# Loading and turning the recurrence's parameters between slots of the first FFN's second stage

## The chip, the cores and the metric

One core of one Trainium2 chip. The metric is the device time of one execution in microseconds. The kernel before took 712.2 us (median of three runs, 710.3 to 714.72).

## The reference

x is [2, 2048, 256] in float32, 4096 tokens. The block is x + 0.5 FFN(ln(x)), then x + recurrence(ln(x)), then x + 0.5 FFN(ln(x)) with the same FFN weights. ln has no gain.

```python
def ffn(x, Wr, br, ln_g, ln_b, W1, b1, W2, b2):      # E = 8 experts, F = 1024
    probs = softmax(x @ Wr + br); gate = max(probs); idx = argmax(probs)
    xn = layernorm(x) * ln_g + ln_b
    h = relu(xn @ W1[idx] + b1[idx])
    return (h @ W2[idx] + b2[idx]) * gate

def recurrence(h, down_w, up_w, layers):             # 3 layers of width 64
    x = h @ down_w.T
    for cw, cb, wr, br, wi, bi, log_a, ow, nw in layers:
        xc = cb + causal_conv4(x, cw)
        r, i = sigmoid(xc @ wr.T + br), sigmoid(xc @ wi.T + bi)
        a = exp(8 * r * log_sigmoid(log_a))
        hs = scan(h = a * h + sqrt(max(1 - a*a, 0)) * i * xc)
        x = rms_norm(hs @ ow.T, nw)
    return x @ up_w.T
```

## The kernel before, in words

The five engines run programs of their own that meet at semaphores. Tokens are routed by expert: for four chunks of 1024 tokens, VectorE takes moments, TensorE the router's logits, VectorE chooses the expert and a place (`choose`, `place`), and POOL scatters the rows with indirect DMAs to regions of DRAM, one per expert (`routed_rows`). A slot is 128 such rows of one expert. The first FFN has up to 40 slots (32 of them always), the second as many again. For each slot SP loads the rows (`slot_rows`, tile pay) and the first-product weights (`slot_weights`, tile w_0 to w_2), VectorE normalises (`norm`), TensorE turns the two halves (`turn_input`), ScalarE applies gain and shift while it keeps them (`affine`, mn_t), TensorE makes the first product in four quarters (`first_product`, 32 instructions), ScalarE and VectorE activate a half each (`activate`), TensorE makes the second product of the slot before (`second_product`), VectorE finishes that (`finish`), and POOL stores it by an indirect DMA. TensorE's order in a slot is: turn the next slot's input, first product, second product of the slot before. In it, a slot's first product must wait for the weights and the affine input, its second for both activations and for VectorE's read of the product before.

The first FFN runs in two stages: slots 0 to 8 need the first two chunks alone, slots 9 and later need all four. Ahead of slot 0 stands the front: loads of x, routing of two chunks, the tables of what each slot holds (`tables`, `order_of_use`), and the third chunk's transposes. The other work is put beside the slots by tables of numbers, `beside(at)`: number k is done in the step k // 24, of which VectorE, ScalarE and POOL have two a slot (before and after its activation) and TensorE eight (after each quarter of a product). The slots of the second stage stand one step of a slot later than their number, so steps 36 and 37 are slot 17's. The recurrence is put beside slots 19 and later of the first FFN and early slots of the second.

The recurrence needs its parameters turned. In the front, SP's `load_parameters` (L412) issues 24 small loads between the large ones, with one expert's second weights (1 MB, L409) after each sixth, all counted by one semaphore, s_par: biases, norm vectors and the slots' own b1, ln_g and ln_b into rows of tile rec that are turned to tile vec; conv_w to lay; six blocks of gate and output weights, down_w and up_w to rec. VectorE zeroes rec for it (L719), waits for all 24 and centres down_w (`centre_down`, L770). TensorE's `parameters` (L1499) waits for all 24, makes the router's product with up_w, and turns 83 rows of vectors, nine blocks of weights, down_w and up_w. ScalarE's `parameters` (L1294) keeps them in vec, rec_t, down_t, up_t and up_r. After it stand the third chunk's logits: `logits` on TensorE, `keep_logits` on ScalarE (tile lg_t, L1330), `turn_logits` on TensorE (L1561), then `in_motion(4)`, products that only keep TensorE busy (L1670), and slot 0.

## Time and profile before

| | us |
|---|---|
| runs, median (lowest to highest) | 712.2 (710.3 to 714.72) |
| profiled execution, first to last instruction | 711.9 |
| TensorE busy | 657.2 |
| VectorE busy | 410.6 |
| ScalarE busy | 272.6 |
| POOL busy | 171.9 |

The profiled execution's own 711.9 us is the span that all rows count from. PE is TensorE's products, PEld its weight loads, DVE is VectorE, ACT ScalarE, SP the queue that issues most DMAs. In a timeline a row is one instruction or several alike (xN): its start, its length, and in brackets the idle time of the engine ahead of it with what ended it. "issue" is idle time with no wait the profile shows, "remote" a wait whose releaser it doesn't know.

### The profile page before, as it was taken

The page shows a single profiled execution, that of the slowest core. Times are in us where ns is not written, and L with a number is a line of the kernel's source. Part 1 is how long each engine was busy: PE and PEld are TensorE (multiplying, and loading weights), DVE is VectorE, ACT ScalarE, POOL GpSimd, SP SyncE. Part 2 cuts the span into 40 slices and gives each one's busy share as a digit, 9 for nine tenths or more (in the row PEclk, how much of TensorE's full clock was granted, in tenths as well). Part 3 has the DMA queues.
Part 4 walks back from the last instruction along what each step waited for, and adds up shares of the span by engine and source line. Part 5 has one row for each costly group of instructions (what it writes and reads, how often), then busy time and mean ns, then how long its engine had stood idle before and what let it go on. Part 6 is the DMA issues. An engine that isn't in the chain of part 4 may idle for free.

```text
span 711.9 us, 15541 instructions
## 1 busy us (share of the span) xinstructions
PE 657.2 (92%) x4420; PEld 576.8 (81%) x4420; DVE 410.6 (58%) x1427; ACT 272.6 (38%) x642; POOL 171.9 (24%) x177
## 2 busy tenths in 40 slices
PE   7549999899999999999998998999899999999993
PEld 5339998899988878898777867889689989999992
DVE  7556772333346586777887767787667633333331
ACT  3124221222245557554562536644443223222220
POOL 4723443011121120123312240124202521111111
PEclk9659999999999999999999999999999999999997
DMA  8969683955564462436416337323373466453530
GB/s 288 307 202 391 242 273 93 322 189 192 180 208 142 149 208 82 150 129 203 148 54 223 123 127 259 135 89 120 127 260 118 166 231 215 150 197 102 175 127 14
DMA packets 59919, 126.51 MB, mean 178 GB/s; under 512 B 8105, under 2 KB 36660, under 8 KB 59700
## 3 DMA queue, kind: packets, MB, share of 16 engines
q1 hardware_dynamic: 53204, 108.50, 45.7%
q0 software_dynamic: 6624, 16.92, 6.5%
q8 instruction: 42, 0.69, 0.4%
q14 instruction: 49, 0.40, 0.2%
HBM read 106.36 MB, written 20.35 MB: 178 GB/s over the span
## 4 chain that ended last, share of the span: by engine, by line
PE 66%; DVE 8%; issue 8%; DMA 6%; DVEq 3%; POOL 3%; another core or an unknown queue 2%; SPq 1%; ACT 1%; POOLq 0%; ACTq 0%
PE bank L1691 30%; PE bank L1705 26%; DMA pay<-routed_rows 3%; POOL routed_rows L633 2%; PE bank L1678 2%; DMA x_middle<-res,pay 2%; PE bank L1595 1%; DMA routed_rows<-rows,dest 1%; DVE st L746 1%; PE bank L1628 1%; PE bank L1533 1%; PE bank L1602 1%; DVE rec L1082 1%; PE bank L1561 1%
## 5 line engine op out<-in xcount | busy, mean ns | idle before, releaser
L1691 PE MATMUL bank<-mn_t,w 128*128 128x128 f32 x2368 | 287.7, 278 | 1.3 <-DVE act_t L1172 1.3
L1691 PEld LDWEIGHTS bank<-mn_t,w 128*128 128x128 f32 x2368 | 277.7, 195 | 11.3 <-issue 8.5
L1705 PE MATMUL bank<-w,act_t 128*128 x1184 | 274.8, 381 | 5.5 <-DVE y_b L1181 5.1
L1705 PEld LDWEIGHTS bank<-w,act_t 128*128 128x128 f32 x1184 | 217.3, 190 | 42.2 <-issue 16.5
L1417 ACT ACTIVATE mn_t<-bank,vec 128x128 f32<-128x128 f32 x152 | 61.4, 454 | 222.3 <-PE bank L1678 198.4
L1172 DVE TENSOR_SCALAR act_t<-bank,vec 128x128 f32<-128x128 f32 x296 | 83.3, 344 | 104.6 <-PE bank L1691 90.4
L1427 ACT ACTIVATE act_t<-bank,vec 128x128 f32<-128x128 f32 x296 | 84.9, 369 | 78.0 <-PE bank L1691 77.9
L642 POOL DMA_INDIRECT x_middle<-res,pay x37 | 36.9, 998 | 220.4 <-DVE res L1188 173.2
L1181 DVE TENSOR_TENSOR y_b<-bank,b_all 128x256 f32<-128x256 f32 x74 | 31.4, 425 | 97.5 <-PE bank L1705 85.4
L642 POOL DMA_INDIRECT out_x<-res,pay x37 | 36.5, 985 | 203.3 <-DVE res L1188 173.3
L633 POOL DMA_INDIRECT routed_rows<-rows,dest x64 | 64.7, 1011 | 55.9 <-PE bank L1691 27.2
L1163 DVE TENSOR_SCALAR mn<-pay 128x256 f32<-128x256 f32 x78 | 32.2, 413 | 21.6 <-DMA pay<-routed_rows 20.9
L625 POOL TENSOR_TENSOR inv_std<-var_eps,minus_half 128x16 f32<-128x16 f32 (+1 forms) x12 | 31.0, 2583 | 50.7 <-DVE var_eps L756 35.5
L1188 DVE SCALAR_TENSOR_TENSOR res<-y_b,pay 128x256 f32<-128x256 f32 x74 | 35.9, 485 | 7.2
L1678 PE MATMUL bank<-ident,mn 128*128 128x128 f32 x152 | 30.5, 283 | 8.2 <-DVE mn L1163 5.9
L746 DVE BATCH_NORM_STATS2 st<-rows 128x6 f32<-128x256 f32 x96 | 33.7, 414 | 2.6 <-DMA rows<-in_L_attn_h 0.7
L1678 PEld LDWEIGHTS bank<-ident,mn 128*128 128x128 f32 x152 | 20.4, 145 | 18.1 <-DVE mn L1163 6.4
L1321 ACT ACTIVATE xn_t<-bank 128x512 f32<-128x512 f32 x32 | 17.9, 600 | 26.9 <-PE bank L1533 20.2
L1058 DVE SCALAR_TENSOR_TENSOR rec<-seq,lay,rec 128x512 f32<-128x512 f32 x36 | 27.0, 749 | 2.0 <-issue 0.2
L1533 PE MATMUL bank<-ident,rows 128*128 128x128 f32 x128 | 20.7, 317 | 0.1
L1561 PE MATMUL bank<-pick,lg_t 128*128 128x16 f32 x64 | 8.9, 271 | 12.4 <-ACT lg_t L1330 12.4
L1359 ACT ACTIVATE rec<-bank,lay 64x512 f32<-64x512 f32 x24 | 16.4, 684 | 9.0 <-PE bank L1595 8.8
(212 smaller groups left out, 465.1 us busy)
## 6 DMA issues: line engine op xcount, KB each, us to landing
w<-in_L_ffn_W SPq DMA_DIRECT2D x82, 1024.0 KB, 7.3
pay<-routed_rows SPq DMA_DIRECT2D x78, 130.0 KB, 2.1
rows<-in_L_attn_h SPq DMA_DIRECT2D x8, 512.0 KB, 6.6
rows<-x_middle SPq DMA_DIRECT2D x8, 512.0 KB, 4.2
routed_rows<-fill SPq DMA_DIRECT2D x2, 1040.0 KB
routed_rows<-rows,dest POOLq DMA_INDIRECT x64
b_all<-in_L_ffn_b SPq DMA_DIRECT2D x1, 1024.0 KB, 10.7
x_middle<-res,pay POOLq DMA_INDIRECT x37, 2.5
```

The source lines that it names most:

```text
L633: g.indirect_dma_start(out=routed[f], out_offset=bass.IndirectOffsetOnAxis(ap=dest[:, t:t + 1], axis=0), in_=rows[:, t * RW:(t + 1) * RW], ...
L642: g.indirect_dma_start(out=x_out if p else x_mid, out_offset=bass.IndirectOffsetOnAxis(ap=pay[p][i % RING][:, C_ID:C_ID + 1].bitcast(I32), ...
L746: v.bn_stats(st[:, jj * 6:jj * 6 + 6], tile_of(c, b, j, 0, D))
L1163: v.tensor_scalar(mn[p][i % 2][:, :], a[:, 0:D], a[:, C_MEAN:C_MEAN + 1], a[:, C_RS:C_RS + 1], ALU.subtract, ALU.mult).then_inc(m_xn[p], 1)
L1172: last = v.tensor_scalar(act_t[i % 2][:, c * P:(c + 1) * P], b_hid[1][:, c % 4 * P:(c % 4 + 1) * P], vec[:, ds(eb + c, 1)], 0.0, ALU.add, ...
L1181: v.tensor_tensor(y_b[i % 2][:, :], b_out[i % 2], b2_all[:, ds(eb * (D // FC), D)], ALU.add).then_inc(m_yk[p], 1)
L1188: v.scalar_tensor_tensor(out=res[p][i % 2][:, :], in0=y_b[i % 2][:, :], scalar=a[:, C_GATE:C_GATE + 1], in1=a[:, 0:D], op0=ALU.mult, op1=A ...
L1417: last = a.activation(mn_t[p][i % 2][:, k * P:(k + 1) * P], b_in[i % 2][:, k * P:(k + 1) * P], ACT.Identity, scale=vec[:, V_G + k:V_G + k ...
L1427: last = a.activation(act_t[i % 2][:, c * P:(c + 1) * P], b_hid[0][:, c * P:(c + 1) * P], ACT.Relu, bias=vec[:, ds(eb + c, 1)])
L1678: last = t.transpose(b_in[i % 2][:, k * P:(k + 1) * P], mn[p][i % 2][:, k * P:(k + 1) * P], ident[:, :])
L1691: last = t.matmul(b_hid[half][:, c % 4 * P:(c % 4 + 1) * P], w1[i % W1S][:, k * F + c * P:k * F + (c + 1) * P], mn_t[p][i % 2][:, k * P:(k ...
L1705: last = t.matmul(b_out[i % 2], act_t[i % 2][:, c * P:(c + 1) * P], w2[:, ds(eb * (WE // FC) + c * D, D)], start=c == 0, stop=c == FC - 1)
```

## The change

Of the 24 loads the front keeps three: b1, ln_g and ln_b, the slots' own. They are turned (68 rows) and kept alone, in columns 0 to 67 of vec. The four experts' second weights are issued behind them in a row. The other 21 loads are issued three at a time by SP behind its work for slots 9 to 15. VectorE zeroes rec behind slot 7's activation and centres down_w behind slot 16's. TensorE turns the parameters between the first and the second quarter of slot 17's first product, into banks 4 to 7, and waits there for all 24 loads. ScalarE keeps them behind slot 17's activation. `layer_columns`, `exp_log_a` and `log_sigmoid` move from slots 0 to 3 to slot 18. The recurrence's first transposes wait for what ScalarE kept.

```diff
@@ -67,3 +67,7 @@
-LAYER_COLUMNS = 2
-EXP_LOG_A = 25
-LOG_SIGMOID = 72
+CLEAR_PARAMETERS = 360
+CENTRE_DOWN = 840
+TURN_PARAMETERS = 3456
+KEEP_PARAMETERS = 888
+LAYER_COLUMNS = 912
+EXP_LOG_A = 936
+LOG_SIGMOID = 937
@@ -215,2 +219,3 @@
-        assert RAW_D + 2 * D + P <= 3 * HC * CH
-        vec_rows = rec[0:NV, 3 * HC * CH - P:3 * HC * CH]
+        assert RAW_D + 2 * D + 2 * P <= 3 * HC * CH and LARGE * 2 <= 3 * HC * CH - P
+        vec_rows = rec[0:E * FC + 2 * KD, 3 * HC * CH - P:3 * HC * CH]
+        layer_rows = rec[0:5 * NL, 3 * HC * CH - 2 * P:3 * HC * CH - P]
@@ -374 +379,3 @@
-        N_PAR = 24
+        N_PAR, PER_SLOT = 21, 3
+        N_SLOT_PAR = 3
+        V_LAYERS = E * FC + 2 * KD
@@ -412 +419,5 @@
-            def load_parameters():
+            def load_slot_parameters():
+                for dst, src in ((vec_rows[0:E * FC, :], b1_in.rearrange("e (c p) -> (e c) p", p=P)),
+                                 (vec_rows[V_G:V_G + KD, :], ln_g.rearrange("(k p) -> k p", p=P)),
+                                 (vec_rows[V_B:V_B + KD, :], ln_b.rearrange("(k p) -> k p", p=P))):
+                    sp.dma_start(dst, src).then_inc(s_par, 16)
@@ -414 +425 @@
-                n_par = [0]
+            def parameter_loads():
@@ -416,9 +426,0 @@
-                def load(dst, src):
-                    sp.dma_start(dst, src).then_inc(s_par, 16)
-                    n_par[0] += 1
-                    if n_par[0] % 6 == 0:
-                        second_weights(n_par[0] // 6 - 1)
-                load(vec_rows[0:E * FC, :], b1_in.rearrange("e (c p) -> (e c) p", p=P))
-                load(vec_rows[V_G:V_G + KD, :], ln_g.rearrange("(k p) -> k p", p=P))
-                load(vec_rows[V_B:V_B + KD, :], ln_b.rearrange("(k p) -> k p", p=P))
@@ -427 +429 @@
-                        load(vec_rows[pos:pos + NL, b * DO:(b + 1) * DO], src)
+                        yield layer_rows[pos - V_LAYERS:pos - V_LAYERS + NL, b * DO:(b + 1) * DO], src
@@ -429,3 +431 @@
-                    load(lay_l[b * DO:(b + 1) * DO, :, 0:4], conv_w.rearrange("l c k -> c l k"))
-                sp.wait_ge(s_zero, 1)
+                    yield lay_l[b * DO:(b + 1) * DO, :, 0:4], conv_w.rearrange("l c k -> c l k")
@@ -435,2 +435,2 @@
-                        load(nat[b * DO:(b + 1) * DO, m, :, b * DO:(b + 1) * DO], src.rearrange("l o i -> o l i"))
-                load(rec[0:DO, RAW_D:RAW_D + D], down_w)
+                        yield nat[b * DO:(b + 1) * DO, m, :, b * DO:(b + 1) * DO], src.rearrange("l o i -> o l i")
+                yield rec[0:DO, RAW_D:RAW_D + D], down_w
@@ -439,2 +439,9 @@
-                    load(upn[:, :, b, :], up_w.rearrange("(k p) i -> p k i", p=P))
-                assert n_par[0] == N_PAR, n_par[0]
+                    yield upn[:, :, b, :], up_w.rearrange("(k p) i -> p k i", p=P)
+            def load_parameters(n):
+                for k, (dst, src) in enumerate(parameter_loads()):
+                    if k == 0 and n == 0:
+                        sp.wait_ge(s_zero, 1)
+                    if n * PER_SLOT <= k < (n + 1) * PER_SLOT:
+                        sp.dma_start(dst, src).then_inc(s_par, 16)
@@ -511,0 +519,2 @@
+                    if FIRST[0][1] <= i < FIRST[0][1] + N_PAR // PER_SLOT:
+                        load_parameters(i - FIRST[0][1])
@@ -565,2 +574,2 @@
-            load_parameters()
-            for e in range(N_PAR // 6, EAGER):
+            load_slot_parameters()
+            for e in range(EAGER):
@@ -719 +727,0 @@
-            v.memset(rec[:, 0:RAW_D], 0.0).then_inc(s_zero, 1)
@@ -771 +779 @@
-                dve.wait_ge(s_par, 16 * N_PAR)
+                dve.wait_ge(s_par, 16 * (N_SLOT_PAR + N_PAR))
@@ -1012,0 +1021,4 @@
+            def clear_parameters():
+                dve.drain()
+                v.memset(rec[:, 0:RAW_D], 0.0).then_inc(s_zero, 1)
@@ -1014 +1026 @@
-                dve.wait_ge(s_tpe, 1)
+                dve.wait_ge(s_tpe, 2)
@@ -1118,0 +1131,4 @@
+                    if k == CLEAR_PARAMETERS:
+                        clear_parameters()
+                    if k == CENTRE_DOWN:
+                        centre_down()
@@ -1277,3 +1293 @@
-            tables(0, 0, 0)
-            centre_down()
-            for part in range(1, 5):
+            for part in range(5):
@@ -1294 +1308 @@
-            def parameters():
+            def slot_parameters():
@@ -1296 +1310,5 @@
-                a.activation(vec[:, :], bank[0][:, 0:NV], ACT.Copy).then_inc(s_tpe, 1)
+                a.activation(vec[:, 0:V_LAYERS], bank[0][:, 0:V_LAYERS], ACT.Copy).then_inc(s_tpe, 1)
+            def parameters():
+                act.wait_ge(s_tp, 2)
+                a.activation(vec[:, V_LAYERS:NV], bk[0][0][:, 0:NV - V_LAYERS], ACT.Copy).then_inc(s_tpe, 1)
@@ -1298,3 +1316,3 @@
-                    a.activation(rec_t[:, m * NL * P:(m + 1) * NL * P], bank[1 + m][:, 0:NL * P], ACT.Copy)
-                a.activation(down_t[:, :], bank[0][:, P:P + KD * DO], ACT.Copy)
-                a.activation(up_t[:, :], bank[0][:, 2 * P:2 * P + D], ACT.Copy)
+                    a.activation(rec_t[:, m * NL * P:(m + 1) * NL * P], bank[5 + m][:, 0:NL * P], ACT.Copy)
+                a.activation(down_t[:, :], bk[0][0][:, P:P + KD * DO], ACT.Copy)
+                a.activation(up_t[:, :], bk[0][0][:, 2 * P:2 * P + D], ACT.Copy)
@@ -1303 +1321 @@
-                                        bank[1][b * DO:(b + 1) * DO, NL * P:NL * P + E], ACT.Copy)
+                                        bk[0][1][b * DO:(b + 1) * DO, NL * P:NL * P + E], ACT.Copy)
@@ -1383,0 +1402,2 @@
+                    if k == KEEP_PARAMETERS:
+                        parameters()
@@ -1488 +1508 @@
-            parameters()
+            slot_parameters()
@@ -1498,0 +1519,4 @@
+            def slot_parameters():
+                pe.wait_ge(s_par, 16 * N_SLOT_PAR)
+                t.transpose(bank[0][:, 0:V_LAYERS], vec_rows, ident[0:V_LAYERS, 0:V_LAYERS]).then_inc(s_tp, 1)
@@ -1500 +1523,0 @@
-                pe.wait_ge(s_par, 16 * N_PAR)
@@ -1501,0 +1525,2 @@
+                pe.wait_ge(s_par, 16 * (N_SLOT_PAR + N_PAR))
+                pe.wait_ge(s_kept[R1], NC)
@@ -1503 +1528 @@
-                    t.matmul(bank[1][:, NL * P:NL * P + E], rec[:, RAW_D + D + k * P:RAW_D + D + (k + 1) * P],
+                    t.matmul(bk[0][1][:, NL * P:NL * P + E], rec[:, RAW_D + D + k * P:RAW_D + D + (k + 1) * P],
@@ -1505 +1530 @@
-                t.transpose(bank[0][:, 0:NV], vec_rows, ident[0:NV, 0:NV])
+                t.transpose(bk[0][0][:, 0:5 * NL], layer_rows, ident[0:5 * NL, 0:5 * NL])
@@ -1509 +1534 @@
-                        t.transpose(bank[1 + m][:, l * P:(l + 1) * P], rec[:, o:o + P], ident[:, :])
+                        t.transpose(bank[5 + m][:, l * P:(l + 1) * P], rec[:, o:o + P], ident[:, :])
@@ -1512 +1537 @@
-                    t.transpose(bank[0][:, P + k * DO:P + (k + 1) * DO], rec[0:DO, RAW_D + k * P:RAW_D + (k + 1) * P],
+                    t.transpose(bk[0][0][:, P + k * DO:P + (k + 1) * DO], rec[0:DO, RAW_D + k * P:RAW_D + (k + 1) * P],
@@ -1515 +1540 @@
-                    last = t.transpose(bank[0][:, 2 * P + k * P:2 * P + (k + 1) * P],
+                    last = t.transpose(bk[0][0][:, 2 * P + k * P:2 * P + (k + 1) * P],
@@ -1520,0 +1546,3 @@
+                if (m, c, part) == (LN, 0, 0):
+                    pe.wait_ge(s_tpe, 3)
@@ -1634,0 +1663,2 @@
+                    if k == TURN_PARAMETERS:
+                        parameters()
@@ -1822 +1852 @@
-            parameters()
+            slot_parameters()
@@ -1825 +1855 @@
-            pe.wait_ge(s_tpe, 2)
+            pe.wait_ge(s_tpe, 1)
```

ScalarE in the front, before, from the third chunk's xn_t to slot 0's mn_t:

```order
L1321 ACTIVATE xn_t<-bank 128x512 [waits transposed0] x3
L1296 ACTIVATE vec<-bank 128x83 [waits param_transposed]
L1298 ACTIVATE rec_t<-bank 128x384 x3
L1299 ACTIVATE down_t<-bank 128x128
L1300 ACTIVATE up_t<-bank 128x256
L1302 ACTIVATE up_r<-bank 64x8 x2
L1330 ACTIVATE lg_t<-bank 128x512 [waits logits0,logits_turned0]
L1417 ACTIVATE mn_t_0<-bank,vec 128x128 [waits slot_transposed0,tables_ready]
```

And now:

```order
L1339 ACTIVATE xn_t<-bank 128x512 [waits transposed0] x3
L1310 ACTIVATE vec<-bank 128x68 [waits param_transposed]
L1348 ACTIVATE lg_t<-bank 128x512 [waits logits0,logits_turned0]
L1437 ACTIVATE mn_t_0<-bank,vec 128x128 [waits slot_transposed0,tables_ready]
L1437 ACTIVATE mn_t_0<-bank,vec 128x128
```

Seven copies have gone from between vec and lg_t.

TensorE at slot 17, before (mn_t_1 and w_2 are its input and first-product weights):

```order
L1678 MATMUL bank<-ident,mn_0 128x128 [waits slot_affine0,slot_normalised0]
L1678 MATMUL bank<-ident,mn_0 128x128
L1691 MATMUL bank<-mn_t_1,w_2 128x128 [waits activated_by_scalar0,slot_weights0_2,slot_affine0]
L1691 MATMUL bank<-mn_t_1,w_2 128x128 x7
L1691 MATMUL bank<-mn_t_1,w_2 128x128 [waits activated_by_vector0]
L1691 MATMUL bank<-mn_t_1,w_2 128x128 x7
L400 TENSOR_LOAD tab_b
```

And now:

```order
L1708 MATMUL bank<-ident,mn_0 128x128 [waits slot_affine0,slot_normalised0]
L1708 MATMUL bank<-ident,mn_0 128x128
L1721 MATMUL bank<-mn_t_1,w_2 128x128 [waits activated_by_scalar0,slot_weights0_2,slot_affine0]
L1721 MATMUL bank<-mn_t_1,w_2 128x128 x3
L1528 MATMUL bank<-wr_c,rec 128x8 [waits counts_kept0,params_loaded]
L1528 MATMUL bank<-wr_c,rec 128x8
L1530 MATMUL bank<-ident,rec 128x15
L1534 MATMUL bank<-ident,rec 128x128 x9
L1537 MATMUL bank<-ident,rec 128x64 [waits down_centred]
L1537 MATMUL bank<-ident,rec 128x64
L1540 MATMUL bank<-ident,rec 128x128 x2
L1721 MATMUL bank<-mn_t_1,w_2 128x128 x4
```

The router's product and the turns stand between the first quarter's four products and the rest, and wait for the loads and for the centring. SP at the end of its work for slot 15 and the start of slot 16's, before (w_0 takes slot 18's weights, pay_4 slot 19's rows, result_stored0_4 counts slot 14's store among others):

```order
L472 ISA [waits first_product_half0]
L472 DMA w_0<-in_L_ffn_W 128x2x1024
L461 TENSOR_LOAD tab_row
L461 ISA x2
L465 ISA [waits result_stored0_4]
L465 DMA pay_4<-routed_rows 128x260
L400 TENSOR_LOAD tab_b
L400 ISA x2
L472 ISA [waits first_product_half0]
```

And now:

```order
L479 ISA [waits first_product_half0]
L479 DMA w_0<-in_L_ffn_W 128x2x1024
L468 TENSOR_LOAD tab_row
L468 ISA x2
L472 ISA [waits result_stored0_4]
L472 DMA pay_4<-routed_rows 128x260
L447 DMA rec<-in_L_attn_down_w 64x256
L447 DMA rec<-in_L_attn_up_w 128x2x64 x2
L407 TENSOR_LOAD tab_b
L407 ISA x2
L479 ISA [waits first_product_half0]
```

The last three of the parameters' loads stand behind the load of slot 19's rows and ahead of slot 19's weights.

## Rows read from the trace of the kernel before

**Rows 1.** The page's head and its busy times by engine

```profile
span 711.9 us, 15541 instructions
...
PE 657.2 (92%) x4420; PEld 576.8 (81%) x4420; DVE 410.6 (58%) x1427; ACT 272.6 (38%) x642; POOL 171.9 (24%) x177
```

**Rows 2.** Busy time by stretch: PE, PEld, DVE, ACT, POOL; clock, DMA share, GB/s

```profile
26.00:42.00 16.00, 4.87 (x26) 3.10 (x26) 5.13 (x25) 1.05 (x2) 10.64 (x11) 0.68 0.69 236
42.00:51.00 9.00, 4.95 (x21) 4.46 (x22) 7.13 (x37) 3.44 (x11) 0.00 (x0) 0.50 0.78 247
51.00:80.00 29.00, 29.00 (x208) 26.87 (x207) 20.82 (x101) 11.29 (x32) 12.83 (x9) 0.92 0.92 330
...
170.00:200.00 30.00, 30.00 (x211) 28.15 (x211) 10.46 (x35) 8.09 (x25) 3.89 (x4) 1.00 0.55 189
```

**Rows 3.** TensorE's timeline in the front: start, us, what, idle before and its releaser

```profile
27.70 0.61 PE L1503 MATMUL bank<-wr_c,rec 128*128 128x8 f32 x4 [2.66 <-DMA rec<-in_L_attn_up_w]
...
30.77 0.69 PE L1515 MATMUL bank<-ident,rec 128*128 128x128 f32 x2
...
45.00 1.89 PE L1561 MATMUL bank<-pick,lg_t 128*128 128x16 f32 x8 [12.39 <-ACT lg_t L1330]
46.72 2.06 PE L1670 MATMUL bank<-ident 128*128 128x128 f32 x8
48.61 0.69 PE L1678 MATMUL bank<-ident,mn 128*128 128x128 f32 x2
...
50.80 1.92 PE L1691 MATMUL bank<-mn_t,w 128*128 128x128 f32 x8
```

**Rows 4.** ScalarE's timeline in the front

```profile
30.84 0.60 ACT L1321 ACTIVATE xn_t<-bank 128x512 f32<-128x512 f32 x1 [4.39 <-remote]
42.28 0.24 ACT L1296 ACTIVATE vec<-bank 128x83 f32<-128x83 f32 x1 [10.84 <-remote]
42.42 1.25 ACT L1298 ACTIVATE rec_t<-bank 128x384 f32<-128x384 f32 x3
...
44.35 0.60 ACT L1330 ACTIVATE lg_t<-bank 128x512 f32<-128x512 f32 x1
```

**Rows 5.** VectorE's timeline in the front

```profile
27.69 0.41 DVE L773 TENSOR_REDUCE mean_d<-rec 64x1 f32<-64x256 f32 x1 [1.56 <-DMA rec<-in_L_attn_up_w]
...
42.13 0.20 DVE L984 TENSOR_TENSOR beyond<-slot_e,jump_v 128x36 f32<-128x36 f32 x1 [2.12 <-issue]
...
48.18 0.38 DVE L1163 TENSOR_SCALAR mn<-pay 128x256 f32<-128x256 f32 x1
```

**Rows 6.** Timelines of POOL and of SP's queue in the front

```profile
38.71 0.98 POOL L633 DMA_INDIRECT routed_rows<-rows,dest  x1 [0.30 <-issue]
...
21.19 0.61 SPq L417 DMA_DIRECT2D rec<-in_L_attn_down_w  x1
21.84 1.15 SPq L417 DMA_DIRECT2D rec<-in_L_attn_up_w  x2
...
42.83 3.65 SPq L465 DMA_DIRECT2D pay<-routed_rows  x4
```

**Rows 7.** Timelines in slots 16, 17 and 19 of the second stage

```profile
176.51 3.74 PE L1691 MATMUL bank<-mn_t,w 128*128 128x128 f32 x32
...
180.40 1.12 DVE L1172 TENSOR_SCALAR act_t<-bank,vec 128x128 f32<-128x128 f32 x4 [2.40 <-PE bank L1691]
180.95 0.35 SPq L465 DMA_DIRECT2D pay<-routed_rows  x1
...
183.76 3.74 PE L1691 MATMUL bank<-mn_t,w 128*128 128x128 f32 x32
183.85 0.42 DVE L1181 TENSOR_TENSOR y_b<-bank,b_all 128x256 f32<-128x256 f32 x1 [2.33 <-PE bank L1705]
...
204.42 1.04 PE L1533 MATMUL bank<-ident,rows 128*128 128x128 f32 x8
```

**Rows 8.** Loads of a slot's rows from 130 to 200 us, issue to landing

```profile
DMA to landing us min/median/max: 2.0/2.1/4.8
```

2 lines of the change are left out of this document (1 added, 1 removed).

## The prediction

> **What bounds the kernel now.** I read the page's totals first, then the busy time by stretch, then the timeline of each engine through the front, and last one slot of the first FFN's second stage. TensorE is busy 657.2 of 711.9 us [rows 1]. By stretch it is full from 51 us on: 29.00 of 29 between 51 and 80, and 30.00 of 30 between 170 and 200, where VectorE works 10.46 and ScalarE 8.09 of the 30 and the DMA engines are 0.55 busy. Between 26 and 42 it works 4.87 of 16 us and from 42 to 51 4.95 of 9 [rows 2]. So there are two prices. An instruction put on TensorE inside the second stage costs its whole length, one put there on VectorE or ScalarE costs nothing while they keep their slack. In the front, only what makes the first slot's work start sooner is worth anything.
>
> What holds that start? TensorE turns the parameters from 27.70 to 31.46, after a wait for the last of 24 small loads, then makes the third chunk's logits, and stands still until 45.00, waiting for ScalarE's lg_t. Then it turns the logits, runs its idle-filling products from 46.72, turns slot 0's input at 48.61 and begins the first product at 50.80 [rows 3]. ScalarE keeps its last xn_t at 30.84, idles 10.84 us for which the profile has no known releaser, copies vec at 42.28 and rec_t from 42.42, and reaches lg_t only at 44.35 [rows 4]. VectorE, beside it, waited 1.56 us for the parameters before centring down_w at 27.69, has gaps of its own (2.12 us before 42.13, by "issue"), and normalises slot 0 at 48.18 [rows 5]. The third string is the rows themselves: POOL issues its last scatter at 38.71, and SP the first loads of slot rows at 42.83 [rows 6].
>
> **The change part by part.**
>
> *Front, ScalarE.* Removed between vec and lg_t: seven copies, from 42.42 to 44.35, 1.93 us [rows 4]. If the 10.84 us stay as they are, lg_t starts at 42.42, 1.9 us sooner, and since turning the logits and the filler follow it with no gap, slot 0's input can be turned at 46.7 [rows 3]. That needs slot 0 normalised by then.
>
> *Front, VectorE.* It loses the 1.56 us wait and centring, two passes of some 0.41 us [rows 5], so 2.4 us; slot 0's norm comes at 45.8 even if every gap stays. Slot 0's rows, issued at 42.83 [rows 6], take 2.1 us in a quiet stretch [rows 8], 44.9. Both are ahead of 46.7. The memset ahead of VectorE's first load wait is gone too, and was hidden by that wait.
>
> *Front, TensorE.* The router product and thirteen turns leave a stretch in which it waits for ScalarE anyway: worth nothing. One transpose, now of 68 rows, stays.
>
> *Front, SP and DMA.* 21 issues leave the queue, the dearest being down_w (0.61) and up_w (1.15 for two) [rows 6]. The first four experts' second weights and the fourth chunk of x are issued back to back. With the small packets gone from among them, these large loads are through a little sooner. That may shorten the unexplained idle of ScalarE and VectorE. The gain of the front has therefore these ends: 0 (the idle of ScalarE grows by what the copies gave back), and 3.2 us where ScalarE no longer matters and the rows do: 42.83 + 2.1 + 0.4 of norm = 45.3 against 48.6. If SP, too, is ready when the last scatter has landed (38.71 + 0.98 + about 2.1 = 41.8, an estimate from rows 6 and 8), another 1.0: 4.2. I take 2.4, near the lower of the two worked cases, 1.9, as ScalarE's idle went on to 42 us while the DMA engines, full at first, were down to 0.69 over 26 to 42 [rows 2].
>
> The Trainium skill would call VectorE's gaps a lock: its page "SBUF — State Buffer", section "SBUF: two separate sides", says VectorE and GpSimd share one port pair, held for a whole instruction, and that descriptors of a GpSimd DMA are written through it. By that rule the gaps last as long as POOL's scatters, which the change doesn't touch, and the gain would be ScalarE's 1.9 alone, the total 712.5. The trace bears it out only in part: VectorE idles 2.12 us up to 42.13, when POOL's last scatter had left it at 39.69, and ScalarE, which has ports of its own, idles longer.
>
> *TensorE's clock.* It ran at the lower of its two levels, 1.2 GHz (granted 0.50), between 42 and 51, after having stood idle, and was at 2.4 GHz for most of 51 to 80 (0.92) [rows 2]. If dense work starts 2 us sooner I let the rise come 2 us sooner with it.
>
> *Second stage, TensorE.* Slot 17 now holds, between its first and second quarter, the router product, one turn of 15 rows, nine of rec, two of down_w and two of up_w. In the front the block took 27.70 to 31.46, 3.76 us, mostly at the lower clock [rows 3], so 1.9 us at the full one; eight transposes of the same shape take 0.9 there [rows 7], which puts the 13 at 1.4 and the rest at 0.4. Ends: 1.7 and 2.2. Nothing hides it, as TensorE has no idle time here. I take 1.9.
>
> *Second stage, the new wait.* That block waits for all 24 loads. Their last three (down_w, up_w twice) stand in SP's program for slot 15, behind the load of slot 19's rows, which waits for slot 14's results to be stored and was issued at 180.95 [rows 7]. The three take 0.61 + 1.15 us to issue [rows 6], so they leave at about 183.15 and land 2.1 later [rows 8], 185.2. TensorE reaches the block a quarter into slot 17's first product: 183.76 + 0.9 = 184.65 [rows 7]. It waits 0.6 us. Ends: 0 (they land with it) and 3.3 (landing takes the 4.8 of the same row). What is queued behind the waiting instruction is the whole of TensorE's work, so each us counts in full.
>
> *Second stage, VectorE.* Centring comes after slot 16's activation, which began at 180.40; VectorE stands in that wait until 185.2, is done at 186.1, and takes slot 15's product at 186.1 and not 183.85 [rows 7]. TensorE wants that product read before its next second product, at about 187.5 (183.76 + 3.74) plus the 2.5 us it is itself late: met. The memset comes after slot 7's activation and the log-sigmoid after slot 18's, both in slack. ScalarE's eight copies come at the end of slot 17, in its slack. Zero for all of these; if that cover failed, 0.8 for the centring and 1.9 for the copies.
>
> *SP in the second stage.* Three issues a slot, at most 1.8 us, delay the first-product weights of three slots ahead by as much. A slot lasts 7.25 us (176.51 to 183.76) [rows 7], and those weights are asked for three slots ahead. Zero.
>
> **The sum**, against the profiled execution's own 711.9 us: -2.4 (front) + 1.9 (the block) + 0.6 (its wait) = +0.1, so 712.0. The median of the runs shown is 712.2, 0.3 from the span, and I leave it at 712.0.
>
> **The rivals.**
>
> *The idle goes with the traffic.* ScalarE's 10.84 us and VectorE's gaps shrink, and only slot 0's rows bound the start. For: they have no releaser in this kernel, and began while the DMA engines were full. Against: they lasted until 42. Gain 4.2: 711.9 - 4.2 + 2.5 = 710.2; with no wait at the block, 709.6.
>
> *The late loads (slower).* TensorE waits at the block not 0.6 but up to 3.3 us. For: in the stretch before, such loads queue behind a megabyte of weights, and SP reaches them only after a wait for a store. Against: here the megabyte is issued before SP's wait for the store, and should be through. With the front's 1.9: 711.9 - 1.9 + 1.9 + 3.3 = 715.2. It decides as soon as the wait is over what the front gave, 0.6 us beyond my figure.
>
> *The idle moves forward (slower).* SP fills the queue from 8 us on, 4 MB of weights with it, and the unexplained idle meets the string moments, choice, placement, on which POOL's first scatter waits. Each us there delays the last scatter and the slot rows. Price between VectorE's 2.12 and half of ScalarE's 10.84 [rows 4, 5], so 2.1 to 5.4, and ScalarE's release would slide with the scatters: 711.9 - 1.9 + 2.5 + 5 = 717.5 at the upper end, 714.6 at the lower. It decides where placement's results come more than 2 us late. Against: the engines were as full before.
>
> *It doesn't do what it says:* ScalarE's idle is a wait that ends at 42 us plus something of the copies' length, so that nothing is gained. 711.9 + 2.5 = 714.4. Little speaks for it.
>
> **How the numbers follow.** Forecast 0.55 (its own range 710.8 to 713.3); idle goes with the traffic 0.2; late loads 0.12; idle moves forward 0.07; nothing gained 0.06. The range reaches from below the first rival to past the late loads: 708.8 to 715.4. The runs shown lie 2 us to either side of their median; 1%, 7.1 us, is about what a measurement of this kernel can tell from no change. No case reaches 705 without a cause I have no row for, 0.04; only the strongest form of the idle moving forward passes 719, 0.04. Within 1%: 0.92.
>
> **What would show it.** Front: in ScalarE's rows lg_t follows vec at once, and TensorE's first slot product begins near 48.4 (right), near 46.6 (first rival), or not before 50 (wrong). Second stage: a new idle time of TensorE ahead of the router product in slot 17, released by up_w's load, of 0.6 us; 3 us would be the second rival, none would lower the time by 0.6. Between slots 16 and 18 TensorE's distance from one first product to the next is 7.25 but for one of 9.8 (7.25 + 1.9 + 0.6). A different length of TensorE's stop between the two stages, or a shift after 260 us that isn't there at 200, would make the account wrong even if the time fits.

## The result, and the profile after

| | before | after |
|---|---|---|
| median of 20 runs, us | 712.13 | 716.86 |
| ratio, 95% interval | 1 | 1.0066 (1.0054 to 1.0078) |
| profiled execution, first to last instruction, us | 711.9 | 715.6 |
| TensorE busy, us | 657.2 | 655.7 |

The changed kernel is 0.66% slower, 4.7 us; one of its 20 runs (1146 us, mean granted clock 0.55 of full speed) is left out of the ratio. Measured once more, beside other versions, it was 1.0055 (1.0034 to 1.0076). 712.0 was predicted, with a range to 715.4.

The page's head and its busy times: TensorE's busy time is no larger; it stands 59.9 us and not 54.7.

```profile
span 715.6 us, 15546 instructions
...
PE 655.7 (92%) x4421; PEld 575.2 (80%) x4421; DVE 410.0 (57%) x1427; ACT 272.0 (38%) x643; POOL 171.9 (24%) x177
```

Busy time by stretch, in the columns of [rows 2]:

```profile
26.00:42.00 16.00, 4.21 (x24) 3.02 (x16) 8.50 (x46) 0.60 (x1) 10.66 (x11) 0.57 0.68 229
42.00:51.00 9.00, 5.03 (x23) 4.66 (x24) 5.46 (x25) 2.44 (x6) 2.61 (x1) 0.50 0.54 154
51.00:80.00 29.00, 29.00 (x210) 26.31 (x210) 17.98 (x82) 9.77 (x29) 11.16 (x10) 0.98 0.98 353
...
170.00:200.00 30.00, 26.81 (x167) 24.78 (x166) 8.40 (x31) 7.76 (x27) 2.92 (x3) 0.89 0.49 159
```

Two stretches differ from [rows 2]. In the front VectorE does 8.50 us of work between 26 and 42 and not 5.13. Between 170 and 200, where TensorE was busy 30.00 of 30 at a granted clock of 1.00, it is busy 26.81 at 0.89.

The front first. Timelines of ScalarE, TensorE, VectorE and SP's queue after, in that order, the answer to [rows 3 to 6]:

```profile
25.59 0.22 ACT L1310 ACTIVATE vec<-bank 128x68 f32<-128x68 f32 x1
26.88 0.60 ACT L1348 ACTIVATE lg_t<-bank 128x512 f32<-128x512 f32 x1 [1.07 <-PE bank L1576]
```

```profile
30.56 2.04 PE L1700 MATMUL bank<-ident 128*128 128x128 f32 x8 [1.68 <-DVE tab_off L964]
44.92 0.69 PE L1708 MATMUL bank<-ident,mn 128*128 128x128 f32 x2 [12.31 <-DVE mn L1179]
...
47.10 1.92 PE L1721 MATMUL bank<-mn_t,w 128*128 128x128 f32 x8
```

```profile
44.45 0.41 DVE L1179 TENSOR_SCALAR mn<-pay 128x256 f32<-128x256 f32 x1 [7.35 <-DMA pay<-routed_rows]
```

```profile
31.40 0.39 SPq L479 DMA_DIRECT2D w<-in_L_ffn_W  x1
42.41 3.65 SPq L472 DMA_DIRECT2D pay<-routed_rows  x4
```

ScalarE's idle of 10.84 us [rows 4] is gone: vec is copied at 25.59 and not 42.28, lg_t at 26.88 and not 44.35. TensorE's wait ahead of slot 0 now ends with VectorE's mn, and VectorE waits for pay, so the slot's rows are the last to come, issued at 42.41 against 42.83 [rows 6]. The first product begins at 47.10, 3.7 us sooner than in [rows 3]: the first rival's mechanism.

Then slot 17. TensorE's timeline after, where [rows 7] had one row of 32 products:

```profile
180.24 0.38 PE L1708 MATMUL bank<-ident,mn 128*128 128x128 f32 x2
180.46 1.06 PE L1721 MATMUL bank<-mn_t,w 128*128 128x128 f32 x8
184.71 0.63 PE L1528 MATMUL bank<-wr_c,rec 128*128 128x8 f32 x4 [3.19 <-DMA rec<-in_L_attn_up_w]
...
187.99 0.69 PE L1540 MATMUL bank<-ident,rec 128*128 128x128 f32 x2
188.47 4.52 PE L1721 MATMUL bank<-mn_t,w 128*128 128x128 f32 x24
...
196.29 0.38 PE L1708 MATMUL bank<-ident,mn 128*128 128x128 f32 x2
```

From one turn of an input to the next it takes 16.05 us (180.24 to 196.29) and not 7.25, so 8.8 too many. 3.4 of them pass between the end of the quarter (some 0.9 after 180.46) and 184.71. The block takes 3.76 (184.71 to 188.47) and the 24 products behind it 4.52 where the same 24 take 2.84 at 2.4 GHz (below): the granted clock has fallen to 1.2 GHz behind the wait (granted 0.56 from 184.7 to 188.4 and 0.59 from 188.5 to 192.8, then 1.00). The chain of what ended last (start, length, what) tells why the loads are late:

```profile
173.82 0.49 DVE res L1204
...
175.06 4.81 DMA x_middle<-res,pay
...
180.04 0.34 SPq L472
...
180.42 1.40 SPq L447
...
181.87 0.59 SPq L447
...
182.50 2.16 DMA rec<-in_L_attn_up_w
...
184.71 0.63 PE bank L1528 x4
```

POOL's store of slot 14's results takes 4.81 us to land; before it was issued at 178.36 and SP's load behind it at 180.95 [rows 7]. There it landed in 2.4 us. SP waits for it ahead of slot 19's rows (L472), and the last three parameter loads (L447) stand behind that.

This is not one unlucky store. The table gives the time from the start of POOL's store to the start of SP's load that waits for it, for six loads of slot rows in a row from 150 us on:

| | us |
|---|---|
| before | 3.07, 2.60, 3.14, 2.59, 2.59, 2.59 |
| after | 4.46, 5.27, 2.58, 4.69, 4.98, 2.58 |

The last of the six stands behind the last parameter load. As long as SP's program has three parameter loads a slot, four stores of five are late. The three issues put SP's weights later: in the stretch above they are issued at 175.76, 0.7 us behind the store's start; before they were issued 3.5 us ahead of it (174.82 and 178.36).

Where is the difference at each point of the program? The start of the turn of each slot's input, minus that of the profile before, for this kernel and for all that were tried (one profiled execution each; "last" is the last turn, at 689.18 before). The profiles are from several chips. Where loads_earlier, turn_later, filler and idle_loads ran, the kernel before itself took 714.58 us (median of 23 runs); beside the other versions it took 711.63 to 712.25, and 712.13 in the measurement above. So in those four rows some 2.5 us can be the chip's, while the ratios, which are taken on one chip, are free of it:

```
                 slot 0   slot 8  slot 11  slot 18  slot 19  slot 20     last
after             -3.69    -2.64    -3.30    -3.30    +5.51    +5.51    +3.66
after_again       -4.31    -3.59    -2.81    -2.81    +2.11    +2.11    +1.70
loads_earlier     -2.41    +1.50    +0.01    +0.01    +2.29    +2.29    +2.59
turn_later        -1.72    +2.44    +0.96    +0.96    +2.32    +4.59    +4.59
both              -3.99    -3.21    -3.05    -3.04    -3.04    -0.77    -0.23
both_again        -4.08    -2.60    -3.75    -3.75    -3.74    -1.47    -3.08
filler            -2.61    -1.38    -2.85    -2.85    +3.09    +3.09    +2.68
act_loads         -3.53    -2.49    -0.96    -0.95    +1.33    +1.32    +1.39
idle_loads        -0.54    +1.31    -0.19    -0.19    +5.89    +5.88    +6.73
idle_rows         -4.14    -1.64    -1.60    -1.59    +3.68    +3.68    +4.28
idle_blocks       -3.99    -2.36    -1.55    -1.54    +5.49    +5.48    +4.19
front_late        -2.90    -0.43    -0.26    -0.25    -0.25    -0.25    -0.71
front_late2       -2.91    -0.41    -0.28    -0.28    -0.27    -0.27    -0.48
```

### The profile page after: what moved, and what is told of

It reads as the page before. It is cut to its first block, busy times and chain, and to the rows that moved or that the text cites. A ratio compares the mean times of both kernels' runs of the same rounds, so it can differ in the third digit from the quotient of the medians.

```text
span 715.6 us, 15546 instructions
## 1 busy us (share of the span) xinstructions
PE 655.7 (92%) x4421; PEld 575.2 (80%) x4421; DVE 410.0 (57%) x1427; ACT 272.0 (38%) x643; POOL 171.9 (24%) x177
## 4 chain that ended last, share of the span: by engine, by line
PE 61%; issue 13%; DVE 8%; POOL 6%; DMA 6%; DVEq 3%; SPq 2%; ACT 1%; POOLq 0%; ACTq 0%
PE bank L1721 27%; PE bank L1735 24%; POOL routed_rows L642 5%; DMA pay<-routed_rows 3%; PE bank L1708 2%; DMA routed_rows<-rows,dest 2%; PE bank L1623 1%; PE bank L1656 1%; PE bank L1561 1%; DVE rec L1094 1%; PE bank L1613 1%; PE bank L1630 1%; DVE st L754 1%; DVE rec L1070 1%; PE bank L1635 1%
## 5 line engine op out<-in xcount | busy, mean ns | idle before, releaser
L1561 PEld LDWEIGHTS bank<-ident,rows 128*128 128x128 f32 x128 | 17.7, 165 | 2.5 <-issue 1.7
```

Source lines behind the costliest of these rows:

```text
L1561: last = t.transpose(bk[cc][n % 2][:, j * P:(j + 1) * P], tile_of(c, b, j, k * P, P), ident[:, :])
```

## The experiments on slot 17

All ratios stand against the kernel before, run on the same chip. Theory: the loss is the stop in slot 17.

**after_again.** No edit.

> The changed kernel once more, unchanged, so that it stands beside the others on one chip. If the loss of 0.66% is the kernel's own, the ratio to the kernel before is again between 1.0045 and 1.009. If part of it was that one chip, it is under 1.004.

Ratio 1.0055 (1.0034 to 1.0076): the loss is the kernel's own. Its profile shows a second way to be late. Chain of what ended last, and TensorE's timeline:

```profile
175.56 2.56 DMA x_middle<-res,pay
...
178.67 0.50 SPq L447
...
179.84 4.49 DMA rec<-in_L_attn_up_w
```

```profile
180.73 0.38 PE L1708 MATMUL bank<-ident,mn 128*128 128x128 f32 x2
...
184.38 0.61 PE L1528 MATMUL bank<-wr_c,rec 128*128 128x8 f32 x4 [2.38 <-DMA rec<-in_L_attn_up_w]
...
186.76 2.84 PE L1721 MATMUL bank<-mn_t,w 128*128 128x128 f32 x24
...
192.89 0.38 PE L1708 MATMUL bank<-ident,mn 128*128 128x128 f32 x2
```

Here the store lands in 2.56 us, SP issues on time, and up_w takes 4.49 to land, with a megabyte of slot weights issued at 177.01 and one more at 181.17. The wait is 2.38 us and the clock stays at 2.4 GHz: block 2.38, slot 12.16, 4.9 too many.

**loads_earlier.** The seven groups of three loads at SP's slots 8 to 14.

```diff
-                    if FIRST[0][1] <= i < FIRST[0][1] + N_PAR // PER_SLOT:
-                        load_parameters(i - FIRST[0][1])
+                    if FIRST[0][1] - 1 <= i < FIRST[0][1] - 1 + N_PAR // PER_SLOT:
+                        load_parameters(i - FIRST[0][1] + 1)
```

> The changed kernel with the 21 loads issued by SP behind its work for slots 8 to 14 and not 9 to 15; nothing else moves. Theory 1 (the loss is the late landing of down_w and up_w: TensorE waits 3.2 us in slot 17, its clock falls, and the turns and the rest of the first product run at the lower clock): the wait and the fall go, 3.2 + 1.9 + 1.8 = 6.9 us less in slot 17, so about 716.9 - 6.9 = 710.0. Rival A (the turns cost as much wherever they stand, and the wait only hides what VectorE or ScalarE would have held up): 714 or more. Rival B (SP's extra issues between the stages delay slots 9 to 12): slots 9 to 12 start later and the time stays over 712.

Ratio 0.9993 (0.997 to 1.0015): the loss is gone. TensorE's timeline in slot 17:

```profile
183.77 1.06 PE L1721 MATMUL bank<-mn_t,w 128*128 128x128 f32 x8
184.66 0.51 PE L1528 MATMUL bank<-wr_c,rec 128*128 128x8 f32 x4
...
186.93 2.84 PE L1721 MATMUL bank<-mn_t,w 128*128 128x128 f32 x24
```

No wait, and the block measured alone: 184.66 to 186.93, 2.27 us. This profile still ends 2.6 us later than the one before, but on this chip the kernel before is itself 2.45 us slower (714.58 against 712.13). The difference arises in the first stage, where TensorE stood at slot 6:

```profile
92.45 3.15 PE L1721 MATMUL bank<-mn_t,w 128*128 128x128 f32 x16 [2.68 <-DVE act_t L1188]
```

VectorE had waited there for a slot's rows (2.00 us for pay at 86.10), whose load SP could issue only when a store had landed.

**turn_later.** The loads stay, everything from the turning on moves back by a slot; centring stays behind slot 16's activation.

```diff
-TURN_PARAMETERS = 3456
-KEEP_PARAMETERS = 888
-LAYER_COLUMNS = 912
-EXP_LOG_A = 936
-LOG_SIGMOID = 937
+TURN_PARAMETERS = 3648
+KEEP_PARAMETERS = 936
+LAYER_COLUMNS = 960
+EXP_LOG_A = 984
+LOG_SIGMOID = 986
```

> The changed kernel with the loads where they are, and TensorE's turns, ScalarE's copies and what follows them one slot later (slot 18); VectorE still centres behind slot 16 and stands there until the loads land. Theory 1: TensorE finds all loads landed, no wait, no fall of the clock, 710 to 710.5, the same as with the loads a slot earlier. Rival A: 714 or more. Rival C (VectorE's own stop behind slot 16, 6.5 us in the changed kernel, is what costs, through slot 15's finish): TensorE waits for y_b in slot 17 and the time is over 713.

Ratio 1.0059 (1.0039 to 1.008), no better than the change. Two timelines tell half of it:

```profile
187.61 0.41 DVE L781 TENSOR_REDUCE mean_d<-rec 64x1 f32<-64x256 f32 x1 [5.13 <-DMA rec<-in_L_attn_up_w]
...
188.88 0.42 DVE L1197 TENSOR_TENSOR y_b<-bank,b_all 128x256 f32<-128x256 f32 x1 [0.35 <-issue]
```

```profile
189.55 3.71 PE L1735 MATMUL bank<-w,act_t 128*128 x16 [1.09 <-DVE y_b L1197]
```

The wait only changed hands: VectorE stands for the same loads, its y_b comes late and TensorE's second product waits for that. That is rival C. Slots 17 and 18 together cost 1.35 + 2.27. That is less than in either profile of the changed kernel, yet the timed runs don't show it: they lie 4.0 us above those of loads_earlier on the same chip (718.67 against 714.70), where the two profiles differ by 2.0 at the last turn. Why the runs are this slow stays open.

**filler.** Fifteen products of the identity with itself, into a bank nobody reads, ahead of the wait.

```diff
-                pe.wait_ge(s_par, 16 * (N_SLOT_PAR + N_PAR))
                 pe.wait_ge(s_kept[R1], NC)
+                for _ in range(15):
+                    t.matmul(bank[6][:, 0:P], ident[:, :], ident[:, :], start=True, stop=True)
+                pe.wait_ge(s_par, 16 * (N_SLOT_PAR + N_PAR))
```

> The changed kernel with 15 products of the identity by itself (30 instructions, 3.3 us, into a bank nobody reads) ahead of the wait for the loads, so that TensorE waits no longer but works. If the fall of the clock is a loss of its own (theory 1), the block takes 1.9 and not 3.8 us and the rest of the first product 2.7 and not 4.5: 3.7 us less, 713.2. If the loss is the wait alone and the rest belongs to the block, no change: 716.9.

In its profile the granted clock is 1.00 between 170 and 200 and slot 17 lasts 13.18 instead of 16.05: the fall was a cost of its own there. The ratio, 1.0076 (1.0049 to 1.0103), is no better than the change's. As after_again shows, the clock doesn't fall in every execution, and the products (3.51 us) outlast a short wait. The profiled execution was also the fastest of its seven (716.40 us, median 719.67), so it says little about the usual one. The forecast 713.2 was missed.

**both.** The two edits together.

> The 21 loads one slot earlier and TensorE's turns (with all that follows them) one slot later. Theory (the loss is TensorE's stop of 3.2 us in slot 17 with the lower clock behind it, 8.8 us in all for a block of 1.9): the loads have landed long before, no TensorE idle time ahead of the router product, the slot with the block lasts 7.25 + 1.9 to 2.3 us, and the ratio is 0.996 to 1.001. Rival (the loads cost what they cost wherever they stand, because SP's three more issues a slot make its weights and rows late): the ratio stays at 1.004 or more, and a slot somewhere between 9 and 20 still lasts 2 us too long besides the one with the block.

Ratio 1.0003 (0.9981 to 1.0024). TensorE's timeline: slot 17 lasts 7.25, slot 18 9.52, without a wait.

```profile
180.50 0.38 PE L1708 MATMUL bank<-ident,mn 128*128 128x128 f32 x2
180.72 3.74 PE L1721 MATMUL bank<-mn_t,w 128*128 128x128 f32 x32
...
187.96 1.06 PE L1721 MATMUL bank<-mn_t,w 128*128 128x128 f32 x8
188.86 0.51 PE L1528 MATMUL bank<-wr_c,rec 128*128 128x8 f32 x4
...
191.13 2.84 PE L1721 MATMUL bank<-mn_t,w 128*128 128x128 f32 x24
```

**act_loads.** ScalarE issues the 21 loads, three behind each activation of slots 9 to 15; SP none.

```diff
+                    if k in range(504, 504 + 48 * 7, 48):
+                        load_parameters((k - 504) // 48)
                     if k == KEEP_PARAMETERS:
                         parameters()
```

(Part of the edit: ScalarE's own copy of the two load functions, and SP's two lines that go, are not shown.)

> The 21 loads are issued by ScalarE behind its activation of slots 9 to 15 (three a slot, as SP did) and not by SP, everything else as in the changed kernel. Theory (SP's queue is what made the last loads late: three more issues a slot push its weights into the store of the results): no wait ahead of the router product in slot 17, slot 17 to 18 lasts about 9.5 us instead of 16, and the ratio is 0.996 to 1.001. Rival one (the small loads disturb whoever else transfers, whichever engine issues them): SP's loads are as late as before and the wait stays near 3 us. Rival two (the issues cost ScalarE, some 0.6 us each, 1.8 a slot): its half of an activation or its affine input comes late and TensorE idles at slots 10 to 16, so the ratio is over 1.003.

Ratio 1.0005 (0.9985 to 1.0025). ScalarE issues its last three at 170.76 to 172.4, SP slot 19's rows at 180.30, and TensorE doesn't wait (slot 17: 9.52). So the parameters' transfers can share the DMA engines; what made them late was their place in SP's order. The edit takes away two things at once, which it doesn't tell apart: the loads' place behind a wait for a store, and the issues that push SP's weights into the stores. From store to load, as in the table above, it is 4.55, 3.72, 3.04, 2.58 and 2.89 us here.

## The experiments on the front

**idle_loads.** The same 21 loads are issued in the front too, in the order of the kernel before, and nothing uses them.

```diff
             load_slot_parameters()
-            for e in range(EAGER):
-                second_weights(e)
+            for n, (dst, src) in enumerate(parameter_loads()):
+                sp.dma_start(dst, src).then_inc(s_idle, 16)
+                if n % 6 == 2:
+                    second_weights(n // 6)
```

(Part of the edit: VectorE waits for these loads behind its tables, and SP ahead of the real ones, so that no tile is written too soon.)

> The changed kernel with the 21 loads issued a second time in the front, in the old order between the second weights, to the same tiles; nobody uses what they bring, and VectorE and SP wait for them before these tiles are written again. It leaves out no work. Asks where the front's gain came from (slot 0's first product at 47.10 and not 50.80, ScalarE's 10.8 us of idle gone). If the small loads make the unexplained idle of ScalarE and VectorE: the idle is back, slot 0's first product begins near 48.9 (ScalarE still free of seven copies), the time about 718.5. If it was the waiting for parameters and the copies: the gaps stay away, slot 0 begins near 47.1, the time 716.9 to 717.3.

Ratio 1.0109 (1.0078 to 1.0141). Timelines of ScalarE, TensorE and VectorE:

```profile
26.60 0.23 ACT L1315 ACTIVATE vec<-bank 128x68 f32<-128x68 f32 x1 [0.84 <-PE bank L1526]
40.16 0.60 ACT L1353 ACTIVATE lg_t<-bank 128x512 f32<-128x512 f32 x1 [13.34 <-remote]
```

```profile
48.07 0.69 PE L1713 MATMUL bank<-ident,mn 128*128 128x128 f32 x2 [3.48 <-DVE mn L1183]
```

```profile
38.79 0.20 DVE L996 TENSOR_TENSOR beyond<-slot_e,jump_v 128x36 f32<-128x36 f32 x1 [1.92 <-issue]
40.19 0.20 DVE L999 SCALAR_TENSOR_TENSOR beyond<-beyond,slot_no 128x36 f32<-128x36 f32 x1 [1.20 <-issue]
41.59 0.19 DVE L1002 TENSOR_REDUCE slot_c<-beyond 128x4 f32<-128x36 f32 x1 [1.20 <-issue]
```

ScalarE's idle is back (13.34 us) with no copy and no parameter to wait for, and so are VectorE's gaps. But the loads are not all of it. On the same chip the three kernels with the changed front and without these loads idle there as well, by 6.30, 5.60 and 6.25 us (loads_earlier, filler, turn_later), with gaps of VectorE of up to 1.9 us. ScalarE in loads_earlier:

```profile
25.63 0.22 ACT L1310 ACTIVATE vec<-bank 128x68 f32<-128x68 f32 x1
32.16 0.60 ACT L1348 ACTIVATE lg_t<-bank 128x512 f32<-128x512 f32 x1 [6.30 <-issue]
```

So the loads lengthen an idle time that can be there without them. Slot 0's input is turned 1.2 to 2.1 us later than in those three, and 3.15 us later than in the changed kernel's profile, which is from another measurement.

**idle_rows and idle_blocks.** The same with the twelve loads of rows and conv_w alone, or with the nine of blocks alone.

```diff
             for n, (dst, src) in enumerate(parameter_loads()):
-                sp.dma_start(dst, src).then_inc(s_idle, 16)
+                if n < 12:
+                    sp.dma_start(dst, src).then_inc(s_idle, 16)
```

(n >= 12 in idle_blocks; the waits as in idle_loads.)

> The changed kernel with only the ten row loads and the two of conv_w (12 loads, packets of 12 to 256 bytes, some 14 KB in all) issued in the front besides, unused; their reloading later stands. With all 21 of them in the front the idle time of ScalarE came back (13.3 us) and slot 0's input was turned at 48.07. Theory A (it is the number of small packets, above all conv_w's, two times 768 bytes by the line in elements of 16 bytes): the idle time comes back with these 12 alone, over 8 us, and slot 0's input is turned after 47. Theory B (it is the blocks of weights, 0.3 MB, by their own traffic): ScalarE's lg_t stays before 30 us and slot 0's input at 45 to 46.

> The changed kernel with only the nine loads of blocks (gate and output weights, down_w, up_w: 0.42 MB in rows of 256 bytes and 1 KB) issued in the front besides, unused. With the twelve small ones alone no idle time came back. Theory (it is the blocks): ScalarE's lg_t comes after 38 us, VectorE's tables are stretched by gaps of 1 to 2 us, slot 0's input is turned after 47. Rival (it takes all 21 together, that is the time at which SP's queue is through with the fourth chunk of x): lg_t before 30 and slot 0's input before 46.

One run each, 717.96 and 717.82 us; the stop in slot 17 is in both (2.73 and 2.94 us). lg_t came at 26.81 and at 28.13, slot 0's input 4.14 and 3.99 us sooner than before: in neither did the idle time come back, against theory A of the first and the theory of the second. Both ran on other chips than idle_loads, and all 21 were not tried there, so that it takes all 21 is not shown. SP was through with the loads of x at 22.0 and 24.9 us, against 26.4 in before and idle_loads; but in loads_earlier it was through at 21.8, and ScalarE idled 6.30.

**front_late.** Loads and turning return to the front, behind the fourth chunk of x and the third chunk's logits; the block in slot 17 goes.

```diff
             load_x(0, 3)
+            for n in range(N_PAR // PER_SLOT):
+                load_parameters(n)
@@
             keep_logits(R1, 2)
+            parameters()
             act.wait_ge(s_tab, 1)
@@
             turn_logits(0, 2)
-            pe.wait_ge(s_tpe, 1)
+            parameters()
+            pe.wait_ge(s_tpe, 3)
```

(Part of the edit: zeroing and centring return to the front with them, the columns' numbers are those of the kernel before, and the turns use the front's banks.)

> The 21 loads and the turning go back to the front, but behind everything: SP issues the loads after the fourth chunk of x (from about 22 us), TensorE turns the parameters behind the third chunk's logits, VectorE centres behind the tables, ScalarE keeps behind lg_t; the block in slot 17 and its wait are gone, and the column work stands in slots 0 to 3 as in the kernel before. In the changed kernel TensorE stands idle from 32.6 to 44.9 us there, VectorE and ScalarE nearly as long, so the block is covered. Theory (what the front lost was lost to the idle time that early blocks of loads bring, and the rest of the loss to slot 17): slot 0's input is turned by 45.5, slot 17 lasts 7.25, and the ratio is 0.994 to 0.998, better than both kernels. Rival (the blocks disturb the front wherever they stand): VectorE and ScalarE idle again between 25 and 42 and slot 0's input is turned after 47.5, ratio 0.998 to 1.003.

Ratio 1.0002 (0.9984 to 1.002). No idle without a known releaser over 1.93 us comes back on ScalarE, and none over 0.43 on VectorE, though all 21 loads are there, issued from 21.8 to 33.6 us; ScalarE waits 11.57 for TensorE's turns and TensorE 5.22 for up_w, both ahead of the slot's rows. Slot 0's input is turned 2.90 us sooner, but at slot 8 only 0.43 of it is left. Idle times and slot 17 (7.25) are as the theory had them, the time is the rival's.

**front_late2.** As front_late, with the column work at slot 18 as in the changed kernel.

```diff
-LAYER_COLUMNS = 2
-EXP_LOG_A = 25
-LOG_SIGMOID = 72
+LAYER_COLUMNS = 912
+EXP_LOG_A = 936
+LOG_SIGMOID = 937
```

> As front_late (loads and turning in the front, behind the third chunk's logits), but with the column work of VectorE and ScalarE (layer_columns, exp_log_a, log_sigmoid) at slot 18, where the changed kernel has it, and no longer in slots 0 to 3, where VectorE is the busiest. In front_late the lead on the kernel before fell from 2.9 us at slot 0 to 0.4 at slot 8. Theory (the column work in the first stage took about 1 us of that, the rest is taken by slot rows that land no sooner than the DMA queues let them): lead at slot 8 between 1 and 2.5, ratio 0.996 to 0.999. Rival (the whole lead goes to the slot rows, whatever VectorE does): lead at slot 8 under 0.6 and the ratio 0.999 to 1.002.

Ratio 0.9989 (0.997 to 1.0009), lead at slot 8 0.41: the rival's figures came, VectorE's column work was not what ate the lead. That slot rows ate it, the rival's other half, is not shown. TensorE's waits in the first stage:

```profile
57.08 1.13 PE L1722 MATMUL bank<-mn_t,w 128*128 128x128 f32 x8 [0.85 <-ACT mn_t L1437]
...
91.15 2.05 PE L1722 MATMUL bank<-mn_t,w 128*128 128x128 f32 x16 [0.50 <-DVE act_t L1187]
...
101.22 3.72 PE L1736 MATMUL bank<-w,act_t 128*128 x16 [0.78 <-DVE y_b L1196]
```

**both_again.**

> The kernel with the loads one slot earlier and the turns one slot later, unchanged, beside front_late2 on one chip. It differs from that one by the block inside slot 18, 2.27 us in its profile, less what the front's loads cost front_late2 (about 1 us of the start). Theory: it is 0.5 to 2 us slower than front_late2, ratio 0.998 to 1.002. Rival (a block in the full second stage costs nothing in the end, since the end of the pass waits for something else): the two are equal within 0.3 us.

Ratio 1.0000 (0.9981 to 1.0019): 0.5 us by the medians (711.9 against 711.42), inside the uncertainty of both, so it doesn't decide. No version tried is faster than the kernel before beyond its uncertainty.

## Why the prediction was wrong

**TensorE's wait, +0.6: the step that failed.** It put the issue of the last three loads at 183.15 and their landing 2.1 us later, and gave 0.6 of wait with an upper end of 3.3. The wait was 3.19 and 2.38 us. Sizes like the 4.8 in [rows 8] decided, not the median 2.1: in one profile for the store that SP waits for (4.81), in the other for up_w itself (4.49). In the first, up_w landed in 2.16 us, at 184.66, sooner than the forecast 185.2. But TensorE stood at the block 3.3 us sooner than forecast (some 181.4 and not 184.65), and the loads did not come sooner by as much: of the 2.8 us that they lack, 2.4 are the store, 4.81 in place of the 2.4 that stood in the 180.95 of [rows 7]. The second rival had sign and place right. loads_earlier, act_loads and both take the wait away, leave the block, and come back to 0.9993 to 1.0005: that shows the wait for these loads to be the cause of the loss. What stays open is turn_later, where TensorE waits 1.09 us and not 3.19 and the runs are no faster.

**"SP in the second stage: zero": wrong.** The three issues a slot don't delay the first products, but they move SP's weights (175.76 in the changed kernel, 174.82 before for the same slot) against a store issued at 175.06 and no longer 178.36. In that profile the store took 4.81 and not 2.4. The table behind the chain shows the same of four stores in five.

**The clock in slot 17: left out.** Behind the 3.19 us wait TensorE ran at 1.2 GHz: the block 3.76 instead of 2.27, the 24 products 1.68 more, together 3.2 us. Behind 2.38 us it didn't. In slot 17 of the three kernels with idle loads it fell behind waits of 2.94 and 1.90 us and not behind one of 2.73, so the length of the wait alone doesn't tell. The upper end of the wait should have carried that with it: 3.3 + 3.2.

**The block, +1.9 (1.7 to 2.2): 2.27.** Right in kind, a little small, and just past its upper end: it was half of the 3.76 us that the block takes at 1.2 GHz, and at 2.4 GHz it takes more than half. both and both_again have the block as their only cost and end equal to the kernel before.

**The front, -2.4 (0 to 4.2): 3.7 at slot 0.** The first rival had the mechanism, but not all of it. In this measurement the idle went with the loads, and the rows bound the start; of the 1.0 us that SP's readiness was to add, 0.4 came (42.41 against 42.83). On the chip of loads_earlier 5.6 to 6.3 us of idle stayed without the loads. But what counts is what is left when the first stage ends, and the prediction took for granted that a lead at slot 0 is a lead at the end. Over the eight profiles with the changed front (after to act_loads in the table) it is 3.3 us at slot 0 on the mean and 2.0 at slot 18, from a loss of 1.0 to a lead of 3.75; without the three from the slower chip it is 3.9 and 2.8. So the 2.4 was near by accident. In the first stage a slot's rows can be loaded only when a store has landed, the DMA engines are 0.98 busy between 51 and 80, and VectorE waits for pay: a slot that starts sooner may find its rows no sooner. That is argued from the rows of loads_earlier and of the changed kernel; no edit tested it.

**The port rule of the Trainium skill** ("SBUF — State Buffer", section "SBUF: two separate sides"), from which the prediction took it that VectorE's gaps would last as long as POOL's scatters: the traces disagree. In the changed kernel POOL's last scatter starts at 38.73 as before, and VectorE has no gap over 0.41 us between 26 and 37, ScalarE none at all that is not a wait for TensorE. In loads_earlier, with the same instructions and scatters in the front, VectorE has gaps of up to 1.85 us, so what these two engines do doesn't settle it.

**The sum, again, from measured sizes:** -2.0 (the lead at slot 18) + 2.27 (block) = +0.3, or -0.5 with the 2.8 of the five profiles. both and both_again measure it as +0.2 and 0.0, each with an interval of some 1.5 us to either side. With the 6.5 and 2.6 us that wait and clock added in the two profiles it is 2.9 to 6.8 (2.1 to 6.0 with the 2.8), around the measured 4.7 and 3.9.

## What to carry to other kernels

A load that the busiest engine waits for must not stand in a queue behind a wait for a store: its time is then the sum of the store's and its own, and one long landing (4.81 or 4.49 us, where 2.4 and 2.1 were reckoned) sets the wait. The issues added to that queue can themselves bring the long landings, as they move what stands behind them. Issuing the loads a slot earlier, or from another engine's queue, brought the 4 to 5 us back; moving the turns a slot later alone did not. And price a gain in the front at the first point where the engine is bound by itself, not where the gain arises: here 30 to 40% of it was gone by slot 18 (3.9 to 2.8 us over five profiles, 3.3 to 2.0 over all eight).

## What the runs showed of the hardware

- With twenty-one small loads, 0.5 MB, issued among megabyte loads and ahead of the last loads of x, ScalarE idled 10.8 and 13.3 us and VectorE's instructions had gaps of up to 2.1 us, until some 20 us after the last of them had been issued (22.99 and 42.28 in the kernel before). Without them both were gone on the chips of the changed kernel, after_again and both_again, but on that of loads_earlier ScalarE still idled 5.6 to 6.3 us. Twelve or nine of them alone did not bring it back, nor did all 21 issued behind the loads of x, in single profiles on other chips. Through what they act isn't known: in the kernel before, instructions were fetched at 23.6, 31.1 and 44.9 us, and none of these transfers (1.2 us at most) ends where ScalarE's idle does.
- Issue to landing of one 64 KB load (up_w) was 2.16 us with the last megabyte issued 6.7 us ahead of it and the next 1.2 us behind, and 4.49 with one issued 2.8 us ahead and one 1.3 us behind. A slot's store took 2.4 us with a megabyte issued 3.5 us ahead of it (before), 2.56 with one issued 1.5 us behind its start, and 4.81 and 5.5 with one issued 0.7 us behind and at its start (after, and after_again at 168.3).
- TensorE's granted clock fell to 1.2 GHz behind idle times of 3.19 us (slot 17), 2.68 us (loads_earlier, slot 6) and 2.33 us (act_loads at 433.9), and stayed at 2.4 GHz behind ones of 2.38 us (after_again, slot 17), 2.73 us (idle_rows, slot 17) and 2.83 us (the changed kernel at 125.7). So the length of the idle time alone doesn't tell.
- ScalarE issued three DMAs behind an activation (0.25 to 0.7 us each) without TensorE waiting for it.
